# Layer 0's attention: the queries' reciprocals eight ticks later on GpSimd, the keys scaled right behind theirs

## The chip, the core and the metric

The kernel runs on one core of a Trainium2 chip. The metric is the device time of one launch in microseconds; lower is better. The engines are TensorE (PE, with its weight loads as PEld), VectorE (DVE), ScalarE (ACT), GpSimd (POOL) and SyncE (SP), which issues the DMAs.

## The reference, cut to what matters

Four transformer layers run over x of shape (16, 256, 128), each an attention and a feed-forward part behind modulated layer norms. The change is in the attention of layer 0: 16 heads of 64, an RMS norm over each head of the queries and keys, a rotation, and causal attention.

```python
def _rmsnorm(x, w):
    rms = jnp.sqrt(jnp.mean(jnp.square(x), axis=-1, keepdims=True) + EPS)
    return x / rms * w
...
q = _rmsnorm(q, q_norm_w)
k = _rmsnorm(k, k_norm_w)
...
q = _rope(q, cos, sin)
k = _rope(k, cos, sin)
scale = D ** (-0.5)
attn = jnp.einsum('bhtd,bhsd->bhts', q, k) * scale
```

## The kernel before

The whole program is one launch. Each engine has its own instruction stream, written out by Python, and the engines meet at counting semaphores. Layer 0's attention is `wide_attention(0, opening)`. Its unit is a block b, one of the 16 batch entries (256 tokens). A block has 8 pairs of heads, and one pair is scored in each tick t, so block b is scored in ticks 8b to 8b+7, and there are 128 scoring ticks.

Work for later blocks is spread over the same ticks. In tick t, with u = t % 8, `a = t//8 + 2` is the block that is projected and rotated, and `b = t//8 + 1` the block whose queries and keys are turned (transposed) for the scores. The pieces of a block are numbered 0 to 7: 0 to 3 are the queries, 4 to 7 the keys, each 128 tokens by 8 heads. Ahead of tick 0 a prologue, `begun`, runs the same steps for blocks 0 and 1.

The way of a piece:
- TensorE projects piece u of block a into PSUM (`tensor_project`).
- VectorE multiplies it with the rotation table, twice (line 727, `q_crossed`), and sums up the squares that ScalarE made of the projection (line 743, `ssq_made`).
- GpSimd adds the halves of the rotation (`gpsimd_add`, lines 991 and 992, `q_rotated`).
- GpSimd makes the reciprocal root of the mean squares, for half a block at a time: `gpsimd_rstd`, a small add (line 998) and a power of 128x32 (line 1000), signalled by `rms_made`. Both halves of block b lie in `SS[b % 3]`.
- The keys' pieces are multiplied with their reciprocals by GpSimd (line 1012, `k_scaled`). The queries are not: their reciprocals enter the row maximum (line 802) and, as a scale, the exponentials (line 947).
- TensorE turns piece u of block b (line 576); for a key piece it waits for `k_scaled`. ScalarE copies it out.

The scores of pair p then go through VectorE's `rowmax` (lines 799, 800, 802), ScalarE's `exps` (line 947), TensorE's `turn` of the probabilities (line 643), the copies (lines 884 and 158) and the product with the values (`value`). GpSimd also adds to the residual (line 172), makes the small reciprocal root of a layer norm (lines 185 and 187, `norm.rstd`, in tick u = 1 of every second block), for which VectorE's normalizing instructions (line 233, u = 3 and 4) wait, and multiplies the outputs by the softmax's reciprocals (line 1026).

The order on GpSimd is that of `gpsimd_tick`, written by hand; each engine runs its instructions strictly in that order. Before the change, the queries' reciprocals of block a are made in u = 6 behind the addition, the keys' reciprocals of block b in u = 0, and key piece n of block b is scaled in u = n - 2.

Of the kernel before, what the change touches and what calls it, by code (L numbers as in the profile page):

```python
# [82 lines left out]
def program(nc, dr, out, stages=STAGES):  # L83
    ctx = ExitStack()
    with ctx:
# [85 lines left out]
        def residual_gpsimd(e, n, tile):  # L171
            e.tensor_tensor(X[:, tile, :], X[:, tile, :], TMP[n % 2], ALU.add).then_inc(added, 1)  # L172
# [233 lines left out]
        q_crossed, ssq_made, rms_made = sem("q_crossed"), sem("ssq_made"), sem("rms_made")  # L406
# [7 lines left out]
        def wide_attention(layer, opening=None):  # L414
# [12 lines left out]
            causal = layer == 0  # L427
# [44 lines left out]
            def posts(t):  # L472

                return [(step, t // 8 - 1) for step, late in (("recip", 0), ("turn", 1), ("scale0", 3), ("scale1", 4), ("c0", 6), ("c1", 7))
                        if t >= 8 and t % 8 == late]

            def normed_in(a):

                if a == -1 or causal and a == 1:
                    return (a + 1) // 2  # L480
                return a // 2 + 1 if 2 * (ahead - 1) <= a < 14 and a % 2 == 0 else None
# [308 lines left out]
            def rowmax(e, p):  # L790

                s, nm, mx = p % 2, NM[p % 2], MX[p % 2]
                e.wait_ge(pair_scored, p0 + p + 1)
                if p >= 2:
                    e.wait_ge(pair_exped, p0 + p - 1)
                if p % 8 == 0:
                    e.wait_ge(rms_made, 2 * (p // 8) + 1)
                two = PALL[:, 1024 * s:1024 * s + 1024].rearrange("p (e x) -> p e x", e=2)
                e.tensor_reduce(mx[:, 0:2], two[:, :, 0:128], AXX, ALU.max, negate=True)
                e.tensor_reduce(mx[:, 2:4], two[:, :, 128:384], AXX, ALU.max, negate=True).then_inc(own_v.sem, own_v.up())  # L800
                e.wait_ge(own_v.sem, own_v.n)
                e.tensor_tensor(nm.rearrange("p (t i) -> p t i", t=2), mx.rearrange("p (t i) -> p t i", t=2), rstd_q(p // 8)[:, :, 2 * (p % 8):2 * (p % 8) + 2],  # L802
                                ALU.mult).then_inc(pair_maxed, 1)

            def rstd_q(b):

                return SS[b % 3][:, 0:32].rearrange("p (t h) -> p t h", t=2)
# [41 lines left out]
            def vector(e):  # L849
# [20 lines left out]
                for t in range(last):  # L870
                    a, b, u = t // 8 + ahead, t // 8 + 1, t % 8
                    vector_project(e, a, u)
                    vector_spread(e, t)
                    vector_extra(e, t, a, b, u)
                    if t < 128:
                        if causal:
                            rowmax(e, t)
                        else:
                            biased_rowmax(e, t)
                    vector_sums(e, t)  # L880
                    if 0 <= t - 1 < 128:
                        ts_writable(e, t - 1)
                        e.wait_ge(pair_turned, p0 + t)
                        e.tensor_copy(*turned_out(t - 1, 0)).then_inc(even_out, 1)  # L884
                    vector_squares(e, a, u)
                    if 0 <= t - guests_at < guest.steps:
                        guest.vector(e, t - guests_at)
# [98 lines left out]
            def gpsimd_add(e, a, u):  # L986

                N = 8 * a + u
                r, c = h3(QR[N % 12]), h3(T2[N % 4])
                e.wait_ge(q_crossed, N + 1)  # L990
                e.tensor_tensor(r[:, :, 0:32], r[:, :, 0:32], c[:, :, 32:64], ALU.add)  # L991
                e.tensor_tensor(r[:, :, 32:64], r[:, :, 32:64], c[:, :, 0:32], ALU.add).then_inc(q_rotated, 1)

            def gpsimd_rstd(e, b, qk):

                half = SS[b % 3][:, 32 * qk:32 * qk + 32]
                e.wait_ge(ssq_made, 8 * b + 4 * qk + 4)
                e.tensor_scalar(half, half, 1.0 / 64, 1e-6, ALU.mult, ALU.add).then_inc(own_g.sem, own_g.up())
                e.wait_ge(own_g.sem, own_g.n)
                e.tensor_tensor(half, half, HALF, ALU.pow).then_inc(rms_made, 1)  # L1000

            def gpsimd_tick(e, t, a, b, u):
                if causal and 0 <= b < 16:
                    if u == 0:
                        gpsimd_rstd(e, b, 1)
                    if 2 <= u < 6:
                        n = u + 2
                        r = h3(QR[(8 * b + n) % 12])
                        if u == 2:
                            e.wait_ge(rms_made, 2 * b + 2)  # L1010
                            e.wait_ge(q_rotated, 8 * b + 8)
                        e.tensor_tensor(r, r, SS[b % 3][:, 8 * n:8 * n + 8].unsqueeze(2).to_broadcast([128, 8, 64]), ALU.mult).then_inc(k_scaled, 1)
                if causal and 0 <= a < 16:
                    gpsimd_add(e, a, u)
                    if u == 6:
                        gpsimd_rstd(e, a, 0)
                if u == 1 and normed_in(a) is not None:
                    norm.rstd(e, normed_in(a))
                for step, c in posts(t):
                    if step in ("scale0", "scale1"):  # L1020
                        half = int(step[5])
                        e.wait_ge(ld_recip, 32 * (b0 + c + 1))
                        for i in (2 * half, 2 * half + 1):
                            k = 4 * c + i
                            e.wait_ge(chunk_out, c0 + k + 1)
                            e.tensor_tensor(OT[k % 6], OT[k % 6], R[:, 2 * i:2 * i + 2, :], ALU.mult).then_inc(chunk_scaled, 1)  # L1026
                    elif step in ("c0", "c1"):
                        qt = 2 * c + int(step[1])
                        s = slots[step, c]
                        e.wait_ge(s.free, s.n)  # L1030
                        residual_gpsimd(e, r0 + qt, qt)

            def gpsimd(e):
                if causal:
                    begun(lambda *at: gpsimd_tick(e, *at))
                for t in range(last):
                    gpsimd_tick(e, t, t // 8 + ahead, t // 8 + 1, t % 8)
                    if 0 <= t - guests_at < guest.steps:
                        guest.gpsimd(e, t - guests_at)
# [26 lines left out]
            def tail_sync(e):  # L1066
# [6 lines left out]
                          lambda e, i: hosted_step(i, lambda *at: vector_prepare(e, *at)),  # L1073
                          lambda e, i: hosted_step(i, lambda *at: scalar_prepare(e, *at)),
                          lambda e, i: hosted_step(i, lambda *at: gpsimd_tick(e, *at)), nothing)
            left = (3, 4, 6, 7)
            tail = Guest(4, lambda i: take_tick(128 + left[i], 16, 17, left[i], ring=BK[6:8]),
# [2236 lines left out]
```

## Time and profile before

| | |
|---|---|
| time, median of 3 runs | 2925.16 us (2923.42 to 2930.45) |
| the profiled execution | 2928.39 us, of which the span is 2925.8 us |
| busy: PE, DVE, ACT, POOL | 94%, 72%, 58%, 36% of the span |
| line 1000 (power of 128x32) | 32 instructions, 5441 ns each, 174.1 us |
| line 1012 (scaling of the keys) in 110 to 590 us | 52 instructions, 1052 ns each |

Layer 0's attention takes about the first 650 us of the span; the prologue reaches to the first row maximum at 66.21 us. All views are of one execution, taken by the profiler. An engine's row in a timeline gives the start, the busy time, the line, the shapes and the count of instructions merged in it, and in brackets the idle time before it with what ended it.

### The profile page before, as it was taken

The numbers are of one execution on the slowest core, as the hardware profiler recorded it, in microseconds if no ns is written. First come the engines' busy times: TensorE is split into PE (matmuls) and PEld (weight loads), VectorE is DVE, ScalarE is ACT, GpSimd is POOL, SyncE is SP. The second block draws the span as 40 slices with busy tenths as digits, with TensorE's granted clock in tenths as the row PEclk, the third lists the DMA queues.
The fourth block names the chain that finished last, engine by engine and source line by source line (L and its number), as shares of the span: only waits on it lengthen the run. The fifth ranks groups of instructions, "written<-read, shape, count | busy, mean of one in ns | idle before, by whom it ended". The sixth has DMA issues, their size and how long they took to land.

```text
span 2925.8 us, 68990 instructions
## 1 busy us (share of the span) xinstructions
PE 2764.6 (94%) x25484; PEld 1864.6 (64%) x25484; DVE 2119.0 (72%) x5801; ACT 1698.9 (58%) x4109; POOL 1042.8 (36%) x1422
## 2 busy tenths in 40 slices
PE   5999999989999999999999799999989988999888
PEld 2666666666666666666666455567767765666666
DVE  6988888865666566666666699855678885887665
ACT  3888888873332367777776477644325544343665
POOL 6888888831000011111111345412243330104441
PEclk9999999999999999999999899999999999999999
DMA  3011111123000011111111554300035443244661
GB/s 106 20 27 31 31 31 31 31 74 102 1 15 1 1 36 31 31 31 30 24 27 27 139 163 131 102 1 15 1 81 173 125 120 78 59 103 128 180 183 37
DMA packets 191996, 186.96 MB, mean 64 GB/s; under 512 B 14528, under 2 KB 168192, under 8 KB 190896
## 3 DMA queue, kind: packets, MB, share of 16 engines
q1 hardware_dynamic: 191664, 182.56, 24.3%
q8 instruction: 205, 3.36, 0.5%
q14 instruction: 127, 1.04, 0.1%
HBM read 129.19 MB, written 53.31 MB: 62 GB/s over the span
## 4 chain that ended last, share of the span: by engine, by line
PE 74%; DVE 10%; ACT 6%; issue 3%; SPq 3%; DMA 2%; POOL 2%; ACTq 0%; DVEq 0%; POOLq 0%
PE pb L161 66%; ACT big L947 4%; PE pb L643 3%; SPq L1869 3%; ACT big L158 2%; DVE big L2198 2%; DVE big L817 2%; PE pb L576 1%; PE pb L2169 1%; DMA parts<-big 1%; PE pb L246 1%; DVE big L233 1%; DMA big<-parts 1%; POOL big L1026 1%; DVE big L727 0%
## 5 line engine op out<-in xcount | busy, mean ns | idle before, releaser
L161 PE MATMUL pb<-big 64*128 64x256 bf16 (+12 forms) x20300 | 2506.4, 329 | 100.2 <-DVE big L2198 33.8
L161 PEld LDWEIGHTS pb<-big 128*128 128x128 f32 (+5 forms) x20300 | 1563.9, 145 | 841.1 <-issue 501.4
L158 ACT ACTIVATE big<-pb 128x512 f32<-128x512 f32 (+7 forms) x1444 | 827.6, 623 | 541.3 <-PE pb L161 311.9
L158 ACT ACTIVATE big<-pb,big 128x512 f32<-128x512 f32 (+2 forms) x536 | 315.5, 616 | 544.5 <-PE pb L161 479.6
L2198 DVE TENSOR_REDUCE big<-pb 128x4 f32<-128x1024 f32 (+1 forms) x256 | 277.7, 1087 | 74.4 <-PE pb L161 69.9
L172 POOL TENSOR_TENSOR big<-big 128x128 f32<-128x128 f32 x192 | 84.8, 456 | 651.8 <-DVE big L169 651.8
L947 ACT ACTIVATE big<-big 128x256 f32<-128x256 f32 x512 | 253.9, 498 | 69.8 <-DVE big L822 68.7
L947 ACT ACTIVATE big<-pb,big 128x128 f32<-128x128 f32 (+1 forms) x512 | 256.6, 525 | 61.2 <-DVE big L802 61.0
L817 DVE CUSTOM_DVE_ANT_0 big<-pb,big 128x256 f32<-128x256 f32 x512 | 186.6, 421 | 100.0 <-PE pb L161 100.0
L1543 DVE SCALAR_TENSOR_TENSOR big<-pb,big 128x128 f32<-128x128 f32 x512 | 144.1, 345 | 138.1 <-PE pb L161 137.4
L1026 POOL TENSOR_TENSOR big<-big 128x512 f32<-128x512 f32 x128 | 159.8, 1275 | 233.4 <-DMA big<-recip 233.4
L1521 DVE SCALAR_TENSOR_TENSOR big<-pb,big 128x512 f32<-128x512 f32 x200 | 148.6, 749 | 89.8 <-PE pb L161 60.6
L185 POOL TENSOR_SCALAR big<-big 128x4 f32<-128x4 f32 (+2 forms) x105 | 27.3, 260 | 495.3 <-DVE big L180 495.3
L643 PEld LDWEIGHTS pb<-big 64*128 64x128 f32 x3584 | 145.3, 139 | 75.9 <-ACT big L947 59.3
L643 PE MATMUL pb<-big 64*128 64x64 f32 x3584 | 157.6, 225 | 26.7 <-ACT big L947 25.5
L1000 POOL TENSOR_TENSOR big<-big 128x32 f32<-128x32 f32 x32 | 174.1, 5441 | 2.7
L727 DVE TENSOR_TENSOR big<-pb,big 128x512 f32<-128x512 f32 x256 | 163.8, 681 | 12.8 <-PE pb L161 9.0
L884 DVE COPY big<-pb 128x384 f32<-128x384 f32 (+1 forms) x256 | 156.9, 613 | 2.3 <-PE pb L643 2.1
L991 POOL TENSOR_TENSOR big<-big 128x256 f32<-128x256 f32 x128 | 83.6, 653 | 85.1 <-DVE big L727 81.9
L576 PEld LDWEIGHTS pb<-big 128*128 128x128 f32 x512 | 63.8, 142 | 76.2 <-issue 66.3
L947 ACT ACTIVATION_READ_ACCUMULATOR big<-pb,big 128x1 f32 x512 | 110.9, 217 | 0.0
L233 DVE TENSOR_SCALAR big<-big 128x128 f32<-128x128 f32 x256 | 96.1, 429 | 8.4 <-POOL big L187 8.3
(147 smaller groups left out, 2192.6 us busy)
## 6 DMA issues: line engine op xcount, KB each, us to landing
big<-parts SPq DMA_DIRECT2D x96, 512.0 KB, 4.1
parts<-big SPq DMA_DIRECT2D x384, 96.0 KB, 2.5
big<-recip SPq DMA_DIRECT2D x64, 512.0 KB, 6.8
big<-comb SPq DMA_DIRECT2D x32, 512.0 KB, 8.2
parts<-big SPq DMA_DIRECT2D x192, 64.0 KB, 2.1
big<-gates SPq DMA_DIRECT2D x7, 1024.0 KB, 6.1
big<-in_wf SPq DMA_DIRECT2D x1, 3072.0 KB, 14.8
big<-scratch SPq DMA_DIRECT2D x1, 3072.0 KB, 17.5
```

The lines of the kernel that those rows point to most:

```text
L158: return e.activation(o, i, f, bias=bias, scale=scale)
L161: return e.matmul(o, l, r_, start=start, stop=stop, skip_group_check=True)
L643: t = e.transpose(banks[2 * (p % 2) + half][:, 64 * at:64 * at + 64], PS[p % 2][rows, i, 128 * blk:128 * blk + 128], IDF[rows, rows])
L727: t = e.tensor_tensor(h3(D), h3(bk), TAB[:, 2 * qk + kk, tile, :].unsqueeze(1).to_broadcast([128, 8, 64]), ALU.mult)
L817: t = e.tensor_tensor_reduce(ps[:, i, x], banks[2 * (p % 2) + i][:, x], U[:, 2 * j + i, 128 - 128 * qt:384 - 128 * qt], 1.0, -3.0e38, ALU. ...
L884: e.tensor_copy(*turned_out(t - 1, 0)).then_inc(even_out, 1)
L947: t = e.activation(ps, banks[2 * s + i][:, at:at + w] if causal else ps, ACT.Exp, bias=NM[s][:, m:m + 1], scale=rstd_q(b)[:, qt, h:h + 1] ...
L1000: e.tensor_tensor(half, half, HALF, ALU.pow).then_inc(rms_made, 1)
L1026: e.tensor_tensor(OT[k % 6], OT[k % 6], R[:, 2 * i:2 * i + 2, :], ALU.mult).then_inc(chunk_scaled, 1)
L1521: e.scalar_tensor_tensor(out=H[n % hn], in0=bk[:, :], scalar=B2[:, nf * u + f:nf * u + f + 1], in1=sg, op0=ALU.add, op1=ALU.mult).then_inc ...
L1543: x = e.scalar_tensor_tensor(out=ACC[s][:, i, :], in0=bk[:, 128 * i:128 * i + 128], scalar=CMB[s][:, E * i + u:E * i + u + 1], in1=ACC[s][ ...
L2198: e.tensor_reduce(m[:, :, 0:n, jj], two[:, :, 0:width].rearrange("p e (q x) -> p e q x", q=n), AXX, ALU.max, negate=True).then_inc(maxed, 1)
```

## The change

The functions compute the same. `gpsimd_rstd` for the queries (second argument 0) is called for block b in u = 6 instead of for block a = b + 1, thus eight ticks later for a given block. The keys of block b are scaled in u = 0 to 3 instead of 2 to 5, behind the keys' `gpsimd_rstd` in u = 0. As the keys' count of `rms_made` now comes before that of the queries of the same block, the counts waited for are exchanged: the scaling waits for 2b + 1, the row maximum for 2b + 2.

```diff
                 if p % 8 == 0:
-                    e.wait_ge(rms_made, 2 * (p // 8) + 1)
+                    e.wait_ge(rms_made, 2 * (p // 8) + 2)
...
                     if u == 0:
                         gpsimd_rstd(e, b, 1)
-                    if 2 <= u < 6:
-                        n = u + 2
+                    if u < 4:
+                        n = u + 4
                         r = h3(QR[(8 * b + n) % 12])
-                        if u == 2:
-                            e.wait_ge(rms_made, 2 * b + 2)
+                        if u == 0:
+                            e.wait_ge(rms_made, 2 * b + 1)
                             e.wait_ge(q_rotated, 8 * b + 8)
...
                 if causal and 0 <= a < 16:
                     gpsimd_add(e, a, u)
-                    if u == 6:
-                        gpsimd_rstd(e, a, 0)
+                if causal and 0 <= b < 16 and u == 6:
+                    gpsimd_rstd(e, b, 0)
```

## Rows read from the trace of the kernel before

**Rows 1.** The page, the chain that ended last by engine.
```profile
PE 74%; DVE 10%; ACT 6%; issue 3%; SPq 3%; DMA 2%; POOL 2%; ACTq 0%; DVEq 0%; POOLq 0%
```
**Rows 2.** Windows: stretch, length, busy time and count by engine, clock, DMA.
```profile
40.00:80.00 40.00, 27.80 (x161) 14.65 (x159) 28.34 (x55) 20.80 (x50) 37.16 (x37) 0.87 0.00 1
...
47.00:48.00 1.00, 0.00 (x0) 0.00 (x0) 0.23 (x1) 0.00 (x0) 1.00 (x2) 0.50 0.00 0
...
110.00:590.00 480.00, 473.04 (x4431) 312.77 (x4428) 419.82 (x851) 393.94 (x1211) 403.59 (x396) 1.00 0.14 29
```
**Rows 3.** Waits, 75 to 590 us: total, times, longest.
```profile
PEld pb L643 <- ACT big L947: 19.5, 40, 1.0
...
PEld pb L576 <- POOL big L992: 4.1, 17, 0.2
```
**Rows 4.** Timeline of GpSimd in the prologue.
```profile
31.54 5.45 POOL L1000 TENSOR_TENSOR big<-big 128x32 f32<-128x32 f32 x1
...
38.60 5.44 POOL L1000 TENSOR_TENSOR big<-big 128x32 f32<-128x32 f32 x1
...
46.71 1.02 POOL L187 TENSOR_TENSOR big<-big 128x4 f32<-128x4 f32 x1
47.71 1.04 POOL L1012 TENSOR_TENSOR big<-big 128x512 f32<-128x512 f32 x1
...
60.64 5.44 POOL L1000 TENSOR_TENSOR big<-big 128x32 f32<-128x32 f32 x1
```
**Rows 5.** Timeline of VectorE in the prologue.
```profile
35.07 0.66 DVE L743 TENSOR_REDUCE big<-big 128x8 f32<-128x512 f32 x1
...
47.77 1.67 DVE L233 TENSOR_SCALAR big<-big 128x128 f32<-128x128 f32 x2 [5.75 <-POOL big L187]
...
51.67 0.69 DVE L787 COPY big<-pb 128x512 f32<-128x512 f32 x1 [0.43 <-PE pb L161]
...
66.21 0.40 DVE L799 TENSOR_REDUCE big<-pb 128x2 f32<-128x256 f32 x1
```
**Rows 6.** Timeline of TensorE in the prologue.
```profile
42.71 1.12 PE L161 MATMUL pb<-big 128*128 128x512 f32 x2 [0.78 <-ACT big L158]
48.81 1.12 PE L576 MATMUL pb<-big 128*128 128x128 f32 x4 [4.97 <-POOL big L1012]
...
51.92 1.72 PE L161 MATMUL pb<-big 128*128 128x512 f32 x2 [0.29 <-ACT big L158]
```
**Rows 7.** Timelines, GpSimd's rstd in tick 6 and VectorE's next block start.
```profile
94.09 5.44 POOL L1000 TENSOR_TENSOR big<-big 128x32 f32<-128x32 f32 x1
...
100.31 0.42 DVE L799 TENSOR_REDUCE big<-pb 128x2 f32<-128x256 f32 x1 [0.48 <-PE pb L161]
...
577.37 0.65 POOL L991 TENSOR_TENSOR big<-big 128x256 f32<-128x256 f32 x1 [2.53 <-DVE big L727]
...
579.01 5.44 POOL L1000 TENSOR_TENSOR big<-big 128x32 f32<-128x32 f32 x1
...
587.91 0.42 DVE L799 TENSOR_REDUCE big<-pb 128x2 f32<-128x256 f32 x1 [0.75 <-PE pb L161]
```
**Rows 8.** Timelines within blocks; the last row: GpSimd by line, 110 to 590 us.
```profile
211.86 5.44 POOL L1000 TENSOR_TENSOR big<-big 128x32 f32<-128x32 f32 x1
...
214.80 0.16 DVE L802 TENSOR_TENSOR big<-big 128x4 f32<-128x4 f32 x1
...
226.90 2.51 POOL L1026 TENSOR_TENSOR big<-big 128x512 f32<-128x512 f32 x2
...
227.48 0.71 DVE L802 TENSOR_TENSOR big<-big 128x4 f32<-128x4 f32 x1
...
230.10 0.20 ACT L947 ACTIVATION_READ_ACCUMULATOR big<-pb,big 128x1 f32 x1
...
230.72 0.53 PE L643 MATMUL pb<-big 64*128 64x64 f32 x12
...
L187 POOL TENSOR_TENSOR big<-big 128x4 f32<-128x4 f32 x5 | 5.1, 1030 | 0.4
```

## The prediction

> **What bounds the kernel now.** I read the profile's page first: TensorE holds 74% of the chain that ended last, GpSimd 2% [rows 1], which are some 58 us of a span of 2925.8. So the question is where in layer 0 GpSimd is waited for at all. The windows answer in two parts [rows 2]. From 110 to 590 us TensorE is busy for 473.0 of 480 us at full clock, while GpSimd is busy for 403.6. From 40 to 80 us TensorE is busy for only 27.8 of 40 us and GpSimd for 37.2: there GpSimd leads. The waits say the same. From 75 to 590 us TensorE's largest wait for another engine is that for ScalarE's exponentials, 19.5 us; for GpSimd there are 17 waits of 0.2 us at most, 4.1 in all, put down to an addition that the turned piece had 8 ticks before [rows 3], so I read them as gaps of TensorE's own. The timeline of the opening shows two engines standing still for it: VectorE 5.75 us before the second normalization, TensorE 4.97 us before the first turn of keys [rows 5, 6].
>
> **What the change moves.** No instruction is added or removed. Per block GpSimd still issues 2 rstd pairs, 4 key scalings, 16 half additions. After the edit the slot behind the addition of piece 6 still holds one rstd of queries, of block b, which is scored 2 ticks later, where it was block b+1, scored 10 ticks later; the slot at piece 0 still holds the keys' rstd. The four key scalings (1.04 us each) move from ticks 2 to 5 to ticks 0 to 3, directly behind the keys' rstd. No DMA moves. No queue but GpSimd's changes, and VectorE's row maximum at each block start now waits for the second count instead of the first.
>
> **The opening, step by step.** Before, the rstd of block 0's queries runs 31.54 to 36.99, so that of its keys begins only at 38.60 [rows 4]. After, the first one is gone from there; but the keys' one needs the squares of piece 7, whose reduction starts on VectorE at 35.07 and takes 0.66, so is ready at 35.73 [rows 5]. I add 0.1 for the signal, 0.30 for the small add ahead of it, and 5.44: it ends at 41.57, against 44.04. That is 2.5 us of the 7.1 us that one slot costs; squares, not GpSimd, are late next. The first scaling follows (0.08 for the signal, 1.04 long) and is done at 42.7, against 48.75 [rows 4]. TensorE, which finishes its projection at 43.83 and now waits until 48.81 [rows 6], turns the keys at once: 5.0 us earlier.
>
> But those 5.0 us do not reach the end of the opening. VectorE waits at line 233 for the rstd of the next normalization (line 187), which stands behind it in GpSimd's queue. Now it ends 3.69 us after the keys' rstd (44.04 to 47.73) [rows 4]; after, the same work stands between, and two scalings as well, 2.1 us with their signal: 41.57 + 3.69 + 2.1 = 47.36, against 47.73. VectorE gains 0.4. Further on it waits 0.43 for TensorE at the copy of values at 51.67 [rows 5], which will be ready some 5 us ahead: 0.4 more, 0.8 in sum. The next projection is released by ScalarE's square, itself behind VectorE, so the 0.8 carries to the first row maximum at 66.21 [rows 5]. There the new wait applies: the queries' rstd sits where the one of 60.64 to 66.08 sits now [rows 4], 0.13 us ahead of the row maximum. Both hang on the same cross product and move together, so I take nothing for it. If the cover is gone, each 0.1 us of lateness costs 0.1 us, once.
>
> TensorE's clock in this stretch is not steady: its mean is 0.87 over 40 to 80 us [rows 2], and the row of 47 to 48 shows 0.50, the 1.2 GHz level, after TensorE had stood still from 43.8 [rows 2, 6]. The two matmuls of a projection took 1.72 us at 51.92, against 1.12 at 42.71 [rows 6]. The new order has an idle stretch of about the same length, from 45 to 51.5, so I price the clock at 0 and keep 2 us to both sides. Opening: bounds -5.0 (everything reaches the end) to +2, value -0.8.
>
> **The steady blocks.** At each block start VectorE now needs an rstd that GpSimd begins in tick 6 of the block before. For block 1 it ends at 99.53 and the row maximum starts at 100.31: 0.78 us to spare. For block 14 it ends at 584.45 against 587.91: 3.46 us [rows 7]. The twelve blocks between have more than that, by the same reading. What hides it is that GpSimd reaches that slot with idle time in front, 2.53 us waiting for VectorE [rows 7], so earlier or later scalings cannot push it. For block 15, GpSimd is without additions and idles anyway. So the wait costs 0; without the cover each microsecond beyond about 4 costs about 14 us over the kernel. The scalings are read at ticks 4 to 7, and being earlier can cost nothing to their reader.
>
> What does change is which GpSimd instruction runs beside VectorE's short ones. The 4-element multiply at line 802, with two SBUF inputs, takes 0.16 us when a 5.44 us power runs beside it, and 0.71 us beside the wide multiply at line 1026, to the end of which it is held [rows 8]. ScalarE's exponentials start on it. In the blocks with a normalization (line 187: five between 110 and 590 us) the line 802 of the block's fourth pair, at 227.48 in the block shown, would meet a new neighbour. GpSimd's queue from the end of the keys' rstd at 217.30 is 4 scalings of 1.0, 4 additions of 1.2 and the normalization's rstd of 1.3, 10.2 us without a pause, so line 1026 starts at about 227.6 instead of 226.90 [rows 8]. If VectorE's multiply falls into line 1026's first piece it is held till 228.9 instead of 228.19: +0.73 us. If it falls before, nothing is lost. The exponentials of this pair end at 230.30 and TensorE turns it at 230.72 [rows 8], 0.4 us of slack, so a part of a loss reaches TensorE here and the rest may at the next pair: five times 0.73 is 3.7 us at most, nothing at least. The two instants, 227.48 and 227.6, are too near each other for my sum to tell them apart, so I take the middle, +1.8. In blocks without a normalization line 802 meets a scaling one tick after the block start and may be held for about half of its 1.04 us. VectorE and ScalarE both meet TensorE's pace again before the block's later pairs, so I take 0, and keep eight times 0.5, 4 us, as the upper bound.
>
> The Trainium skill ("SBUF — State Buffer", Who interferes with whom) states that a VectorE instruction with two SBUF inputs and a GpSimd instruction that reads SBUF exclude each other, and that the loser blocks for the whole instruction. For line 1026 the trace agrees (0.71 us); for the power it doesn't: 0.16 us in the middle of 5.44 [rows 8]. Taken whole, the rule would put the sum at the upper end, the 3.7 us, and make +2.9 of +1.0.
>
> **Sum.** -0.8 + 1.8 = +1.0 us. The profiled execution took 2928.39 us (span 2925.8), so it would take 2929.4; the median of the runs, 2925.16, lies 3.2 below it, and there the forecast is 2926.1 us.
>
> **Rivals.**
> 1. Small terms as above, 2926: chance 0.50. For it: GpSimd's re-synchronisation by VectorE before tick 6 [rows 7].
> 2. The port collisions cost their full 3.7 us: 2925.16 - 0.8 + 3.7 = 2928. For it: line 802's 0.71 us [rows 8]. Against it: the power that doesn't block. 0.20.
> 3. The 5.0 us of TensorE's wait at the keys reach the end: 2920. For it: TensorE's wait at 48.81 [rows 6]. Against it: VectorE's wait for line 187, 5.75 us at the same time [rows 5]. 0.12.
> 4. The change does nothing that counts, the opening's gain being lost at the first exponentials or to the clock: 2925. 0.11.
> 5. Slower: the row maximum at each block start waits for the queries' rstd. It decides where GpSimd's slot in tick 6 slips by more than 3.5 to 5 us; at 1 us beyond, 14 us, 2939. Against it: the 2.53 us of idle time before it, on each block [rows 7]. 0.04.
> 6. Much faster: TensorE's waits for exponentials in the blocks (19.5 us) are GpSimd's doing through line 802 and the new order clears half of them: 2915. Against it: at the block starts, where GpSimd's order stays, line 802 is short already [rows 8]. 0.03.
>
> Rivals 1 to 4 lie within 0.3% of the median (8.8 us, about what a measurement of this kernel can tell from no change). So faster by over 0.3%: 0.03; within: 0.93; slower: 0.04. The range takes in rivals 1, 2 and 4 and the lower one at its edge, with the spread of the runs shown (2923.4 to 2930.5): 2920 to 2931; both upper bounds together, 2932, lie just outside.
>
> **What would show it.** After, GpSimd's keys' rstd of block 0 starts near 36.1, the first turn of keys near 43.8, VectorE's line 233 near 47.4 still with a wait for line 187, and the first row maximum near 65.4. In the blocks the rstd in tick 6 keeps its place, and no row has VectorE's line 799 waiting on GpSimd's line 1000; line 802 at pair 35 is the one to look at. The prediction is wrong if line 799 waits for line 1000 on every block, or if the period of a block, 37.5 us on average, moves by over 0.6 us.

## The result, and the profile after

| | before | after |
|---|---|---|
| median of 20 runs | 2925.61 us (2921.96 to 2933.01) | 2930.20 us (2924.25 to 2935.65) |
| ratio | | 1.0014, 95% interval 1.0007 to 1.0020 |
| span of the profiled execution | 2925.8 us | 2926.2 us |

The changed kernel is slower by 0.14% by the ratio, which is 4.1 us, with 2.0 to 5.9 us by the interval; the medians differ by 4.6 us. That is within the 0.3% that the forecast called no change, and inside its range; the forecast was +1.0 us. The two profiled executions differ by only 0.4 us in span. The last row maximum comes 5.95 us later after the change (656.45 against 650.50), but the rest of the program, which is the same in both, took 2269.7 us instead of 2275.3. In the eleven profiles of this document that rest lies between 2269.7 and 2279.4 us, so spans cannot show the loss; the stretches of layer 0 can.

The prologue went as worked out in its first steps. The timeline of GpSimd after, answering to [rows 4]:

```profile
36.28 0.22 POOL L998 TENSOR_SCALAR big<-big 128x32 f32<-128x32 f32 x1 [2.90 <-DVE big L743]
36.59 5.45 POOL L1000 TENSOR_TENSOR big<-big 128x32 f32<-128x32 f32 x1
42.12 1.05 POOL L1012 TENSOR_TENSOR big<-big 128x512 f32<-128x512 f32 x1
...
46.84 1.03 POOL L187 TENSOR_TENSOR big<-big 128x4 f32<-128x4 f32 x1
...
60.93 5.44 POOL L1000 TENSOR_TENSOR big<-big 128x32 f32<-128x32 f32 x1
```

and of VectorE and TensorE, answering to [rows 5, 6]:

```profile
35.54 0.65 DVE L743 TENSOR_REDUCE big<-big 128x8 f32<-128x512 f32 x1
...
47.90 1.66 DVE L233 TENSOR_SCALAR big<-big 128x128 f32<-128x128 f32 x2 [5.41 <-POOL big L187]
...
51.87 1.09 DVE L233 TENSOR_SCALAR big<-big 128x128 f32<-128x128 f32 x2
52.89 0.67 DVE L743 TENSOR_REDUCE big<-big 128x8 f32<-128x512 f32 x1
54.24 1.29 DVE L727 TENSOR_TENSOR big<-pb,big 128x512 f32<-128x512 f32 x2 [0.68 <-PE pb L161]
...
57.92 1.29 DVE L727 TENSOR_TENSOR big<-pb,big 128x512 f32<-128x512 f32 x2 [1.80 <-PE pb L161]
...
66.53 0.39 DVE L799 TENSOR_REDUCE big<-pb 128x2 f32<-128x256 f32 x1
...
44.13 0.60 PE L576 MATMUL pb<-big 128*128 128x128 f32 x4
...
52.04 2.07 PE L161 MATMUL pb<-big 128*128 128x512 f32 x2 [6.44 <-ACT big L158]
...
54.75 3.03 PE L161 MATMUL pb<-big 128*128 128x512 f32 x4
```

GpSimd now waits for the squares (2.90 us), TensorE turns the first keys at 44.13 instead of 48.81, and VectorE stands still at line 233 as before, for 5.41 us. The first row maximum comes at 66.53, not earlier. TensorE's idle stretch is 6.44 us long, and the clock (third number from the end of a row, columns as in [rows 2]) is at half in what follows it:

```profile
46.00:48.00 2.00, 0.00 (x0) 0.00 (x0) 0.10 (x1) 0.00 (x0) 1.92 (x4) 1.00 0.00 0
50.00:52.00 2.00, 0.00 (x0) 0.00 (x0) 2.00 (x5) 0.60 (x1) 2.00 (x4) 0.56 0.00 0
52.00:54.00 2.00, 1.96 (x3) 0.82 (x4) 1.56 (x3) 0.00 (x0) 1.49 (x3) 0.50 0.00 0
```

The block starts, answering to [rows 7]: the rstd still starts behind 2.5 us of idle time, and VectorE's row maximum waits for TensorE, not for it.

```profile
95.14 5.44 POOL L1000 TENSOR_TENSOR big<-big 128x32 f32<-128x32 f32 x1
...
101.54 0.42 DVE L799 TENSOR_REDUCE big<-pb 128x2 f32<-128x256 f32 x1 [0.48 <-PE pb L161]
...
581.07 0.64 POOL L991 TENSOR_TENSOR big<-big 128x256 f32<-128x256 f32 x1 [2.52 <-DVE big L727]
...
582.70 5.44 POOL L1000 TENSOR_TENSOR big<-big 128x32 f32<-128x32 f32 x1
...
591.61 0.42 DVE L799 TENSOR_REDUCE big<-pb 128x2 f32<-128x256 f32 x1 [0.75 <-PE pb L161]
```

The row maximum of pair 112 is 3.7 us later than before, and the delay grows in steps. The stretch from row maximum 16 to 24 holds a normalization. Its two ends before:

```profile
138.58 0.40 DVE L799 TENSOR_REDUCE big<-pb 128x2 f32<-128x256 f32 x1
...
175.28 0.42 DVE L799 TENSOR_REDUCE big<-pb 128x2 f32<-128x256 f32 x1 [0.29 <-PE pb L161]
```

and after:

```profile
139.78 0.39 DVE L799 TENSOR_REDUCE big<-pb 128x2 f32<-128x256 f32 x1
...
177.12 0.42 DVE L799 TENSOR_REDUCE big<-pb 128x2 f32<-128x256 f32 x1 [0.28 <-PE pb L161]
```

36.70 us became 37.34. Inside such a stretch (the one of [rows 8]) the timelines after show where:

```profile
227.18 1.05 POOL L1012 TENSOR_TENSOR big<-big 128x512 f32<-128x512 f32 x1
...
229.39 2.50 POOL L1026 TENSOR_TENSOR big<-big 128x512 f32<-128x512 f32 x2
...
227.23 1.69 DVE L233 TENSOR_SCALAR big<-big 128x128 f32<-128x128 f32 x2
228.84 0.41 DVE L799 TENSOR_REDUCE big<-pb 128x2 f32<-128x256 f32 x1
...
229.88 0.79 DVE L802 TENSOR_TENSOR big<-big 128x4 f32<-128x4 f32 x1
...
232.84 0.59 PE L643 MATMUL pb<-big 64*128 64x64 f32 x12 [0.17 <-ACT big L947]
```

VectorE's normalizing pair at line 233 starts 0.05 us after GpSimd's last scaling (line 1012) and takes 1.69 us; before, the pair at the same place took 0.94:

```profile
225.47 0.94 DVE L233 TENSOR_SCALAR big<-big 128x128 f32<-128x128 f32 x2
```

Line 802 took 0.79 against 0.71 [rows 8]. So the row maximum is late, the exponentials behind it are too, and TensorE has a gap of 0.17 us before the turn of the probabilities (line 643), where it had none [rows 8].

### The profile page after: what moved, and what is told of

Same layout as the page of the kernel before. It is cut to its first block, busy times and chain, and to the rows that moved or that the text cites. A ratio compares the mean times of both kernels' runs of the same rounds, so it can differ in the third digit from the quotient of the medians.

```text
span 2926.2 us, 68990 instructions
## 1 busy us (share of the span) xinstructions
PE 2767.5 (95%) x25484; PEld 1865.5 (64%) x25484; DVE 2122.7 (73%) x5801; ACT 1700.9 (58%) x4109; POOL 1044.4 (36%) x1422
## 3 DMA queue, kind: packets, MB, share of 16 engines
q8 instruction: 205, 3.36, 0.5%
## 4 chain that ended last, share of the span: by engine, by line
PE 73%; DVE 11%; ACT 6%; issue 3%; POOL 2%; SPq 2%; DMA 2%; ACTq 0%; DVEq 0%; POOLq 0%
PE pb L161 66%; ACT big L947 4%; PE pb L643 3%; ACT big L158 2%; DVE big L2198 2%; DVE big L817 2%; SPq L1869 2%; PE pb L576 1%; PE pb L2169 1%; DVE big L233 1%; PE pb L246 1%; DVE big L727 1%; DVE big L2699 1%; DMA parts<-big 1%; DVE big L800 1%
```

## The experiments

Each ran together with the kernel before, on the same chip, in three groups: e1 to e4, e5 to e7, e8 and e9. The medians of the kernel before in these groups are 2926.6, 2924.9 and 2927.2 us, so it is the ratios that compare across them. Two theories were put to the test. Theory 1: the last scaling, which now runs beside line 233, holds it. Theory 2: the new wait of the row maximum, for an rstd due only 2 ticks ahead, costs the time. The table is worked out from the starts of line 799 in each profile, in us. Its columns are the first row maximum; the stretch from pair 0 to 8; the stretch from 8 to 16; the five later stretches with a normalization (from pair 16, 32, 48, 64 and 80, eight pairs each) in sum; and the row maximum of pair 112.

| kernel | ratio (95%) | first | 0 to 8 | 8 to 16 | five, sum | pair 112 |
|---|---|---|---|---|---|---|
| before | | 66.21 | 34.10 | 38.26 | 183.8 | 587.91 |
| after | 1.0014 (1.0007 to 1.0020) | 66.53 | 35.00 | 38.25 | 186.7 | 591.61 |
| e1, scalings alone | 1.0026 (1.0016 to 1.0036) | 69.57 | 34.14 | 39.50 | 186.8 | 594.96 |
| e2, rstd alone | 0.9992 (0.9980 to 1.0003) | 63.23 | 32.88 | 38.13 | 184.8 | 584.17 |
| e3, last scaling behind | 1.0011 (1.0003 to 1.0020) | 66.45 | 34.62 | 40.70 | 183.0 | 589.36 |
| e4, after + normalizing later | 0.9986 (0.9975 to 0.9997) | 60.75 | 33.65 | 41.81 | 183.0 | 584.99 |
| e5, e2 + normalizing later | 0.9991 (0.9981 to 1.0000) | 65.11 | 32.80 | 38.14 | 184.1 | 584.81 |
| e6, before + normalizing later | 0.9988 (0.9979 to 0.9998) | 65.86 | 34.53 | 38.15 | 184.1 | 587.10 |
| e7, after again | 1.0010 (1.0000 to 1.0020) | 66.64 | 35.02 | 40.68 | 186.8 | 594.39 |
| e8, block 2 in old ticks | 1.0005 (0.9995 to 1.0015) | 66.04 | 35.02 | 38.11 | 186.8 | 590.99 |
| e9, normalization blocks too | 1.0002 (0.9991 to 1.0013) | 66.32 | 32.45 | 38.26 | 184.4 | 586.49 |

The first row maxima need a correction. The executions are already apart when line 743 first runs, near 21 us, ahead of anything that the edits reach, and by the same amount at the line 743 near 35 us. Against the kernel before (35.07) that one starts later by 0.47 us after the change, 0.55 in e1, 0.05 in e2, 0.09 in e3, 0.21 in e5, 0.34 in e7, 0.29 in e8 and 0.12 in e9, and earlier by 0.70 in e4 and 0.33 in e6. "Net" below means with this taken off.

**e1, the scalings alone.** To the kernel before:

```diff
-                    if 2 <= u < 6:
-                        n = u + 2
+                    if u < 4:
+                        n = u + 4
...
-                        if u == 2:
+                        if u == 0:
                             e.wait_ge(rms_made, 2 * b + 2)
```

> Only the scalings of the keys move to ticks 0 to 3; the queries' rstd stays where it was before the change, and with it the wait. Theory 1 (VectorE's normalizing instruction, line 233, is held by the last scaling beside it): the block with a normalization takes 37.3 us from row maximum 16 to row maximum 24, as after the change (before: 36.7), and the first of the two normalizing instructions takes 1.07 us. Theory 2 (the row maximum's later wait, or the rstd now due 2 ticks ahead, costs it): 36.7 us. In the prologue both expect the second normalization's rstd 2.1 us later than before the change (two scalings more ahead of it), so the first row maximum near 68 us. Time: theory 1 about 2930 to 2931, theory 2 about 2927.

Measured: five stretches of 186.8, as after. Line 233 by its own view (counts, then shortest, median and longest in ns, from 110 to 450 us), before, e1 and after:

```profile
L233 DVE TENSOR_SCALAR big<-big x16: 331/504/685, 150.3 to 382.3; 128x128 f32<-128x128 f32 x16
```
```profile
L233 DVE TENSOR_SCALAR big<-big x16: 328/681/1083, 154.9 to 389.1; 128x128 f32<-128x128 f32 x16
```
```profile
L233 DVE TENSOR_SCALAR big<-big x16: 331/680/1077, 151.4 to 385.6; 128x128 f32<-128x128 f32 x16
```

The longest went from 0.69 to 1.08 us wherever the scalings moved, with the queries' rstd untouched. Theory 2 expected 36.7 us from pair 16 to 24; it took 37.34. The prologue is worse than expected (69.57, expected near 68; net 2.8 us behind the kernel before), and the time, 2935.5 us, is more than expected.

**e2, the rstd alone.** To the changed kernel: the scalings back in `2 <= u < 6` with `n = u + 2`, their wait for `2 * b + 1` in `u == 2`.

> Only the queries' rstd moves, eight ticks later, with the wait of the row maximum; the scalings stay in ticks 2 to 5. Theory 1: the block from row maximum 16 to 24 takes 36.7 us, as before the change; theory 2: 37.3 us. In the prologue nothing stands between the keys' rstd and the second normalization's rstd but two additions, so that rstd should end near 45.7 us and the first row maximum come 1.5 to 2 us sooner, near 64.6 us. Time: theory 1 about 2924, theory 2 about 2928.

The new wait is all here, and the stretches are 184.8, 1.0 above before (in two of them line 802 of the fourth pair was held 1.24 us) against 2.9 after. The prologue gained 3.0 us, more than expected. TensorE's clock was at full speed from 40 us on, where before and after it was at 0.87 in the mean; its stretch at half speed came earlier in this execution, from 34 us:

```profile
34.00:36.00 2.00, 1.20 (x5) 1.24 (x6) 1.97 (x11) 0.68 (x2) 0.13 (x1) 0.60 0.00 0
36.00:38.00 2.00, 1.84 (x4) 0.29 (x4) 1.87 (x4) 1.12 (x2) 1.92 (x2) 0.55 0.00 0
40.00:80.00 40.00, 29.05 (x202) 15.84 (x202) 32.79 (x64) 23.93 (x61) 37.60 (x41) 1.00 0.00 1
```

**e3, the last scaling behind the addition.** To the changed kernel: `if u < 3` for the first three, and the fourth after `gpsimd_add`:

```diff
                     gpsimd_add(e, a, u)
+                if causal and 0 <= b < 16 and u == 3:
+                    r = h3(QR[(8 * b + 7) % 12])
+                    e.tensor_tensor(r, r, SS[b % 3][:, 56:64].unsqueeze(2).to_broadcast([128, 8, 64]), ALU.mult).then_inc(k_scaled, 1)
```

> The changed kernel, with the scaling of piece 7 issued behind the addition of tick 3 instead of ahead of it. Theory 1: line 233 no longer meets a scaling and takes 0.34 us for its first instruction instead of 1.07; the block from row maximum 16 to 24 takes 36.7 to 36.9 us. Theory 2: it stays at 37.3. The prologue stays as after the change (first row maximum near 66.5). Time: theory 1 about 2927, theory 2 about 2930.

The stretches fell to 183.0, below those before, and line 233 at this place took 0.93 us for two:

```profile
228.46 0.93 DVE L233 TENSOR_SCALAR big<-big 128x128 f32<-128x128 f32 x2
```

So one instruction's place makes the difference of 3.7 us over five stretches. But the time did not fall as expected (2931.0 us, expected 2927). One reason stands in the table: 40.70 us from pair 8 to 16, where line 802 once took 3.38 us (see e7).

**e4, VectorE's normalizing a tick later.** To the changed kernel:

```diff
-                    elif u in (3, 4):
-                        norm.normed(e, c, 2 * u - 6, 2 * u - 4)
+                    elif u in ((4, 5) if causal else (3, 4)):
+                        i0 = 2 * u - (8 if causal else 6)
+                        norm.normed(e, c, i0, i0 + 2)
```

> The changed kernel with VectorE's two normalizing steps in ticks 4 and 5 instead of 3 and 4, so beside other instructions of GpSimd's. Theory 1: no normalizing instruction of a block is held by a scaling, and the block from row maximum 16 to 24 takes 36.7 us or a little less, since tick 5 has slack. Theory 2: 37.3 us. In the prologue VectorE meets its wait for the rstd one tick later, so the first row maximum is no later than 66.5 us. Time: theory 1 about 2925 to 2927, theory 2 about 2930.

Again 183.0: leaving GpSimd's order and moving VectorE's half of the collision does the same. The first row maximum came 5.5 us sooner than before, net 4.8. The median, 2922.9 us, is the lowest of all, but the ratio of 0.9986 is not told apart from those of e2, e5 and e6 (0.9988 to 0.9992): the intervals overlap. In the prologue VectorE's wait for line 187 shrank to 1.57 us, and the clock is full throughout:

```profile
46.75 1.66 DVE L233 TENSOR_SCALAR big<-big 128x128 f32<-128x128 f32 x2 [1.57 <-POOL big L187]
...
60.75 0.42 DVE L800 TENSOR_REDUCE big<-pb 128x2 f32<-128x256 f32 x1
```
```profile
40.00:80.00 40.00, 30.41 (x213) 17.00 (x212) 33.43 (x66) 25.21 (x64) 38.54 (x43) 1.00 0.00 1
```

(Line numbers are one higher in this kernel: L800 is the row maximum.)

**e5 and e6.** e5 is e2 with e4's edit; e6 is the kernel before with e4's edit.

> The queries' rstd eight ticks later, the scalings left in ticks 2 to 5, and VectorE's normalizing steps in ticks 4 and 5. If the gain of the earlier rstd in the prologue was stopped by VectorE's wait for the normalization's rstd, this one passes it on: first row maximum near 60 to 62 us (before the change 66.2). Blocks with a normalization 36.6 us, and none of the others above its value before the change. If instead the prologue is held by TensorE's clock, the first row maximum stays near 63. Time 2919 to 2922, so a ratio near 0.998.

> The kernel before the change with VectorE's normalizing steps in ticks 4 and 5, nothing else. If the prologue is bound by the two rstds in a row on GpSimd, taking VectorE's wait away gives little: first row maximum 65 to 66.2 us. If VectorE's place of waiting alone is what counts, it comes near 61. Blocks with a normalization 36.6 to 36.7. Time 2924 to 2926.

e6's first row maximum is 65.86, 0.35 us sooner, but this execution was 0.33 ahead already at line 743. So VectorE's place of waiting alone is worth nothing there: before the change the two rstds in a row bind. Still, e6's ratio is 0.9988, and what made it faster its profile does not show (0.8 us at pair 112). e5 missed its 60 to 62: 65.11, net 1.3 us sooner. Two things differ from e4. The keys are scaled later, so TensorE turns the first ones at 46.59 instead of 42.97. And the clock is at half for two stretches, 0.83 in the mean. e2 turned the keys as late (46.43) and had full clock then, so the two are not told apart. e5's median, 2923.7 us, is above the 2919 to 2922 expected, and its ratio no better than e2's.

```profile
46.59 1.11 PE L576 MATMUL pb<-big 128*128 128x128 f32 x4 [2.54 <-POOL big L1013]
```
```profile
40.00:80.00 40.00, 32.67 (x176) 17.45 (x175) 29.66 (x60) 22.43 (x58) 37.20 (x40) 0.83 0.00 1
```

**e7, the changed kernel again**, unaltered, for a second profile.

> The changed kernel once more, as a second profile of the same program. What the order of the instructions causes comes again: blocks with a normalization 37.3 us, first normalizing instruction 1.07 us, first row maximum 66.0 to 66.6. What only the one execution had may not: the last eight scoring ticks were 2.4 us longer than before the change, with TensorE at the lower clock in part of them. Time 2928 to 2932.

The stretches with a normalization repeat to 0.1 us in sum, the one from 0 to 8 and the first row maximum too. The end of the layer, from row maximum 120 to 127, was 2.4 us longer than before in the first profile and is 2.0 us shorter in this one: that difference was the execution's, not the order's. New is 40.68 us from pair 8 to 16. GpSimd there, then VectorE:

```profile
115.52 0.67 POOL L991 TENSOR_TENSOR big<-big 128x256 f32<-128x256 f32 x1
116.12 0.67 POOL L992 TENSOR_TENSOR big<-big 128x256 f32<-128x256 f32 x1
116.73 2.51 POOL L1026 TENSOR_TENSOR big<-big 128x512 f32<-128x512 f32 x2
...
115.92 3.33 DVE L802 TENSOR_TENSOR big<-big 128x4 f32<-128x4 f32 x1
```

and VectorE in the first profile of the same program:

```profile
115.82 0.24 DVE L802 TENSOR_TENSOR big<-big 128x4 f32<-128x4 f32 x1
```

The 4-element multiply fell at nearly the same point of the same queue. Once it got in after the running addition; once it stood through four instructions of GpSimd's.

**e8 and e9.** The changed kernel with `d = 2` for some blocks, else 0:

```diff
-                    if u < 4:
-                        n = u + 4
+                    d = 2 if b == 2 else 0
+                    if d <= u < d + 4:
+                        n = u + 4 - d
...
-                        if u == 0:
+                        if u == d:
```

e9 has `if b == 2 or b % 2 == 1`.

> The changed kernel, with the scalings of block 2 alone (made in ticks 8 to 15) back in ticks 2 to 5 of the eight. In the second profile of the changed kernel the stretch from row maximum 8 to 16 took 40.7 us, with one 4-element multiply (line 802) held for 3.33 us by four instructions of GpSimd's in a row; in its first profile 38.25 with no such hold. If the hold comes from the scalings filling GpSimd's pauses, this stretch takes 38.1 to 38.3 us here and no line 802 takes over 1.3 us in it; the blocks with a normalization stay at 37.3. If it comes by chance or from the rstd's new place, it may be 40 us or more. Time 2927 to 2930.

> The changed kernel, with the scalings of block 2 and of all odd blocks (those made beside a normalization) back in ticks 2 to 5; even blocks and the prologue as changed. Theory 1: the stretches with a normalization are back at 36.7 us (row maximum 16 to 24), the first normalizing instruction at 0.33 us, the stretch from row maximum 8 to 16 at 38.2; what is left of the change is the prologue, row maximum 0 near 66.5, and the time is that of before the change, 2925 to 2926, ratio 1.000 within 0.001. If the loss had another source (the row maximum's wait, the scalings of the even blocks), the time stays near 2930.

e8: 38.11 us from pair 8 to 16, no long hold, the other stretches as after. Its time, 2928.3 us against 2927.2, does not show the loss on its own: the interval of the ratio reaches from 0.9995 to 1.0015. e9: the five stretches come back to 184.4, line 233 to 0.68 at most, and the time to 2927.7 us against 2927.2, ratio 1.0002:

```profile
L233 DVE TENSOR_SCALAR big<-big x16: 331/506/680, 148.7 to 381.0; 128x128 f32<-128x128 f32 x16
```

The stretch from 0 to 8 fell from 35.02 in e8 to 32.45 in e9, but only part of this is block 1's scalings. TensorE's clock was not the same in it, 0.95 in e8 and 1.00 in e9:

```profile
66.04:101.06 35.02, 32.78 (x294) 19.95 (x294) 31.73 (x63) 29.88 (x93) 27.31 (x28) 0.95 0.01 2
```
```profile
66.32:98.77 32.45, 31.48 (x296) 19.70 (x298) 30.79 (x63) 29.60 (x93) 26.66 (x27) 1.00 0.01 2
```

e9 keeps the late rstd, its wait, the changed prologue and the early scalings of the even blocks other than block 2. None of these costs anything that can be measured here; the interval leaves room for 3.8 us.

## Why the prediction was right, and where it was off

**The prologue, -0.8: the mechanism held, the size did not.** The keys' rstd ended at 42.04 (forecast 41.57), VectorE went on at 47.90 (47.44) and TensorE turned the keys at 44.13 (43.8). All three are 0.3 to 0.5 us late, because this execution started its work at line 743 0.47 us later than before, ahead of anything that was changed. Taking this off, the first row maximum gained 0.15 us, not 0.8. The other three executions with the same prologue give +0.1 (e7), -0.5 (e8) and 0.0 (e9), none of them -0.8. The step that failed is the price of 0 for the clock. I had called TensorE's new idle stretch, 45 to 51.5, about as long as the old one; by my own figures it was 6.5 us against 5.0, and it measured 6.44. At line 743 behind the second normalizing pair VectorE was 0.90 us ahead of before (52.89 against 53.79). Of this, 0.5 I had not counted: that pair took 1.09 us against 1.59. Then VectorE lost it to TensorE, which ran at half clock. The projection at 52.04 took 2.07 us where I had reckoned with 1.72, and VectorE waited 0.68 us for it; the four matmuls at 54.75 took 3.03 us, and VectorE waited 1.80 us at 57.92, where it had waited 1.35 at 57.61. The spread of first row maxima at full clock (60.75, 63.23) and below (65.11, 66.53) goes the same way, but the kernels differ in order too, so that the clock alone makes it is argued and not shown.

**The 5.0 us that do not reach the end.** Right, and for the reason given: line 187, two scalings later, holds VectorE. e4 takes that wait one tick further on and gets net 4.8 us, at full clock; e6 shows that without the moved rstd this buys nothing. How much of the 4.8 is the wait and how much the clock is not told apart. Rival 3 needs a second edit.

**The new wait costs 0.** Right: no row has line 799 waiting for GpSimd, in any of the profiles, and e2 and e9, which keep the wait, lose nothing measurable.

**Port collisions, +1.8, bounds 0 to 3.7: mis-sized and put on the wrong instruction.** The five stretches lost 2.9 us. Every order with these scalings in the old ticks gives 183.8 to 184.8 us (before, e2, e5, e6, e9), every one with them early and neither neighbour moved 186.7 to 186.8 (after, e1, e7, e8). I had looked at line 802 against line 1026, and asked whether it starts before or after the edge of line 1026's first piece. It started 0.49 us inside (229.88 against 229.39) where it had been 0.58 inside (227.48 against 226.90): both had moved together, and it took 0.79 against 0.71. The loss is at line 233, one instruction pair earlier, against the last scaling. By my own sum that scaling would start at 225.4 (227.6 less an addition of 1.2 and a scaling of 1.0), and VectorE's pair stood at 225.47. I did not compare the two instants. In the first stretch, 0 to 8, which I had left out, another 0.9 us went. Here the clock counts as well. At a mean clock of 0.95 this stretch took 34.10 and 34.53 us with block 1's scalings in the old ticks (before, e6) and 35.00 to 35.02 with them early (after, e7, e8); at 0.98 to 1.00 it took 32.45 to 32.88 (e2, e5, e9) and 33.65 to 34.14 (e1, e4). So the early scalings cost something at either clock, between 0.5 and 1.7 us (e3, with the last one moved, had 34.62 at 0.95), and the rest of e9's gain goes with the clock.

**Not foreseen: the long hold.** It lengthened stretch 8 to 16 by 2.4 to 3.6 us in e3, e4 and e7 (line 802 took 3.38, 3.36 and 3.33 us) and by 1.2 in e1 (2.52 us), in the first profile of the changed kernel not at all, and in none of the six kernels (before, e2, e5, e6, e8, e9) that have block 2's scalings in the old ticks. Why one multiply gets in and another does not, within 0.1 us of the same point, stays open. Early scalings leave GpSimd fewer pauses there; that this is the cause fits e8, but e8 is one profile, and the first profile of the changed kernel had no hold either, so it is not shown.

**The sum.** Five stretches +2.9, the first +0.9, the prologue +0.3 with its late start, the other stretches up to pair 112 -0.4: 3.7 us; with the hold of e7, +2.4 more, 6.1. The measured 4.6 lies between. Rival 2 (2928, the collisions at full price) was the nearest case; it had 0.20. That the time fell inside the range is partly luck: the 1.8 us was the middle between nothing and 3.7 us at line 802, which in the block shown lost 0.08, and the loss that took its place came at an instruction that I had not priced. The period of a block between pairs 8 and 112 moved by 0.2 us on average (37.51 to 37.70; 37.90 in e7), within the 0.6 that I had allowed, while in the blocks with a normalization it moved by 0.6. One sum in the prediction does not come out: the upper bounds of +2 and 3.7 us make 2930.9, not 2932, and with the 4 us for the other blocks 2934.9.

## What to carry to other kernels

When instructions of GpSimd are moved, list which VectorE instructions stand beside them at the new place, not only who waits for whom; the collision cost 0.6 us a block although no semaphore changed for it. A wait that ends 5 us sooner is worth what the next engine's wait leaves of it; look whether that next wait can be moved behind work that needn't have it (e4, whose first row maximum came 4.8 us sooner where the change alone gave 0.15). For effects of 0.1%, sums over repeated stretches of one profile can settle what the total time cannot, if the clock was the same in them and if the start of a chain is compared at a point ahead of the edit.

## What the runs showed of the hardware

A VectorE instruction may be held by GpSimd for more than the one running: 3.33 us for a multiply of 0.16, over four of GpSimd's in a row, in one execution and not in another of the same program. A 5.44 us power on 128x32 beside it holds it not at all: line 802 took 0.16 or 0.17 us in each of the 31 places before the change where it started well inside such a power. The Trainium skill ("SBUF — State Buffer", Who interferes with whom) says that the loser blocks for the whole instruction. Line 233 behind a scaling agrees (1.07 us against 0.33, ending with the scaling); the power does not, and the hold over four goes beyond it.
